# Layer 3's attention: scores and transposed probabilities share two alternating PSUM banks, and the tasks of a step run in another sequence

## The chip, the cores and the metric

The kernel runs on one core of one Trainium2 chip. The metric is the device time of one execution in microseconds (us). Six engine rows appear in the profile: PE (TensorE's matmuls), PEld (its weight loads), DVE (VectorE), ACT (ScalarE), POOL (GpSimd) and SP (which issues the transfers).

## The reference, cut to what matters

The program is a four-layer network over 16 batches of 128 tokens and 256 channels. The change touches layer 3's attention alone. It has two passes: `own` (keys and values from the tokens themselves) and `cross` (keys and values from a context). Each pass computes, for each batch:

```python
q = ln(fp8_linear(ln_out, wq))       # 16 heads of 128
k = ln(fp8_linear(ln_out, wk))       # 8 key heads of 128
v = fp8_linear(ln_out, wv)           # 8 value heads of 128
scores = einsum("bsghd,btgd->bghst", q, k) * d ** -0.5
p = softmax(scores)
core = einsum("bghst,btgd->bsghd", p, v)
x = x + fp8_round(core / proj_smooth) @ wproj * scale
```

In the cross pass k and v come from `cond @ w_kv_x` in float32. What follows layer 3's attention (a mixture of experts) starts when the cross pass has ended.

## The kernel before, in words

`stage_l3_attention` runs `Layer3Pass` twice, own and cross, each with a block of its own on all engines. A pass goes through its 16 batches in **steps**. One step works on four batches at once: `a`, the attention of batch n; `c`, centring, transposing and scaling the heads of batch n+1 and projecting its values; `p`, projecting queries and keys of batch n+2 and taking their statistics; `r`, rounding the rows of batch n+3. `steps` (L2882) gives each engine the tasks of one hand-written list, `OWN_ORDER` (L2735) or `CROSS_ORDER` (L2757), in the order of that list: an engine runs those that are its own, strictly in sequence, and waits on semaphores inside each. There are three steps that only fill the pipeline, then twelve in a hardware loop of two steps a turn (batches 0 to 11 at `a`), one more full one (batch 12), and then one without `r`, one without `p` as well, and one with `a` alone: 16 steps have an attention batch.

The attention of a batch is cut into four units u of four heads each. The chain of one unit goes: `scores` (L3030, PE, 8 matmuls into the PSUM bank `s_ps`), `maximum` (L3257, DVE), `exponential` (L3103, ACT, four heads), `normalise` (L3261, DVE), `turn_probs` (L3043, PE, four transposes into the bank `pt_ps`), `turned` (L3137, ACT, a copy to SBUF), `apply` (L3050, PE), `scale` (L3142, ACT), `round` (L3270, DVE, five instructions), `output` (L3058, PE, 12 matmuls). After four units `add` (L3281, DVE) adds the result to X. As there is one bank of each kind, scores of unit u wait for the exponential of unit u-1, and the transposes of unit u for `turned` of unit u-1:

```python
wait(pe, exp_ready, at_batch(b, U, u))        # scores
wait(pe, probst_ready, at_batch(b, U, u))     # turn_probs
```

The other tasks: `project` and `project_values` (L2989, L3005, PE into `p_ps`, two banks), `keep` and `keep_values` (L3113, L3119, ACT), `statistics` (L3227, DVE, four heads), `deviation` (L3232, DVE; it waits for the last centring of the batch before), `inverse` (L2944, POOL, a power and a product), `center` (L2952, POOL, five units of four heads), `center here` (L3249, DVE, the sixth unit), `turn_heads` (L3012, PE), `affine` (L3126, ACT), and in the own pass `rows`, `magic` and `quantise` (L3200, L3205, L3210, DVE) and `value` (L3083, ACT). In the own pass's last two steps `next weights` (L3164 and L3306) cuts eight tiles of the cross pass's weights into two parts each, ACT first, then DVE; SP loads a tile (`sp_load`, L2697) into one of two buffers when the tile two before it has been cut.

Of the kernel before, what the change touches and what calls it, by code (L numbers as in the profile page):

```python
# [22 lines left out]
P = 128  # L23
# [2700 lines left out]
class Layer3Pass:  # L2724
# [20 lines left out]
        ("a", "normalise", 2), ("p", "keep", 3), ("a", "scores", 3), ("a", "next weights", 1), ("a", "turn", 2),  # L2745
# [3 lines left out]
        ("a", "round", 1), ("c", "affine", 1), ("a", "next weights", 2), ("a", "apply", 2), ("p", "statistics", 3),  # L2749
# [7 lines left out]
    CROSS_ORDER = [  # L2757
        ("a", "scores", 0), ("a", "exponential", 0), ("a", "maximum", 0), ("c", "project values", 0),
        ("c", "keep values", 0), ("a", "normalise", 0), ("c", "project values", 1), ("c", "center", 0),
        ("c", "keep values", 1), ("a", "maximum", 1), ("a", "scores", 1), ("r", "value", 0), ("a", "turn", 0),  # L2760
        ("r", "quantise", 0), ("a", "turned", 0), ("p", "project", 0), ("a", "exponential", 1),
        ("c", "center here", 2), ("a", "apply", 0), ("p", "keep", 0), ("a", "normalise", 1), ("p", "project", 1),
# [704 lines left out]
```

## Time and profile before

| what | before |
|---|---|
| median of 3 runs (lowest to highest) | 2794.41 us (2784.98 to 2795.93) |
| the profiled execution | 2789.37 us, span 2787.6 us |
| PE busy over the span | 2289.0 us (82%) |
| DVE, ACT, POOL busy | 1831.1 (66%), 1524.3 (55%), 1515.2 us (54%) |
| last `add` of the own pass's batch 15 | at 1859.2 us of the span |
| last `add` of the cross pass's batch 15 | at 2335.7 us of the span |

The profile shows one execution; times in it count from the first instruction. Busy time counts what an engine executes, not its waits. In a timeline, idle time before an instruction is put down to what released it. The two passes of layer 3's attention lie between about 1325 and 2340 us.

### The profile page before, as it was taken

The page shows a single profiled execution, that of the slowest core. Times are in us where ns is not written, and L with a number is a line of the kernel's source. Part 1 is how long each engine was busy: PE and PEld are TensorE (multiplying, and loading weights), DVE is VectorE, ACT ScalarE, POOL GpSimd, SP SyncE. Part 2 cuts the span into 40 slices and gives each one's busy share as a digit, 9 for nine tenths or more (in the row PEclk, how much of TensorE's full clock was granted, in tenths as well). Part 3 has the DMA queues.
Part 4 walks back from the last instruction along what each step waited for, and adds up shares of the span by engine and source line. Part 5 has one row for each costly group of instructions (what it writes and reads, how often), then busy time and mean ns, then how long its engine had stood idle before and what let it go on. Part 6 is the DMA issues. An engine that isn't in the chain of part 4 may idle for free. (4 is left out here: it accounts for less than half of the span.)

```text
span 2787.6 us, 45731 instructions
## 1 busy us (share of the span) xinstructions
PE 2289.0 (82%) x14565; PEld 1664.4 (60%) x14574; DVE 1831.1 (66%) x3797; ACT 1524.3 (55%) x3405; POOL 1515.2 (54%) x1497
## 2 busy tenths in 40 slices
PE   4898244969889586897389999868999997999998
PEld 2333022548546343785267777757888886788886
DVE  3887585655547354455678888757888874666565
ACT  1677383752120265343478888757788773344443
POOL 5542104520002442583278888818888882888882
PEclk9999665989999799799699999988999996999999
DMA  5243103432040443232200000020000000343443
GB/s 135 68 97 69 50 0 91 148 121 110 4 187 1 105 93 89 84 101 68 94 1 0 0 0 0 7 78 7 4 6 6 2 2 30 100 116 111 117 115 82
DMA packets 119445, 174.20 MB, mean 62 GB/s; under 512 B 25597, under 2 KB 79005, under 8 KB 116207
## 3 DMA queue, kind: packets, MB, share of 16 engines
q1 hardware_dynamic: 118703, 171.58, 21.7%
q8 instruction: 91, 1.49, 0.2%
q10 hardware_dynamic: 576, 0.52, 0.1%
q14 instruction: 75, 0.61, 0.1%
HBM read 122.06 MB, written 11.48 MB: 48 GB/s over the span
## 5 line engine op out<-in xcount | busy, mean ns | idle before, releaser
L527 DVE TENSOR_REDUCE a_mraw<-a_wave_ps 128x4 f32<-128x1024 f32 (+1 forms) x256 | 308.4, 1218 | 118.6 <-PE a_wave_ps L359 115.2
L415 ACT ACTIVATE a_et<-a_wave_ps 128x1024 f32<-128x1024 f32 x256 | 262.9, 1028 | 113.9 <-PE a_wave_ps L376 110.6
L2956 POOL TENSOR_SCALAR a3o_raw<-a3o_raw,a3o_mu,a3o_dev 128x128 f32<-128x128 f32 x320 | 304.8, 967 | 5.4 <-issue 5.4
L2956 POOL TENSOR_SCALAR a3x_raw<-a3x_raw,a3x_mu,a3x_dev 128x128 f32<-128x128 f32 x320 | 280.2, 891 | 4.8 <-issue 4.8
L1755 DVE TENSOR_TENSOR f3e_hidden_low<-f3e_hidden,f3e_hidden_high 128x512 fp32r<-128x512 f32 x96 | 116.6, 1215 | 126.6 <-ACT f3e_hidden_high L1708 126.2
L393 PE MATMUL a_o_ps<-a_et,a_vt 128*32 128x256 f32 x2048 | 167.3, 400 | 26.1 <-ACT a_osb L445 24.4
L1616 POOL TENSOR_TENSOR f3e_product<-f3e_silu,f3e_up 128x512 f32<-128x512 f32 x96 | 143.6, 1499 | 72.0 <-PE f3e_u_ps L1635 43.0
L359 PE MATMUL a_wave_ps<-a_ks,a_qs 64*128 64x256 bf16 (+2 forms) x1280 | 121.3, 267 | 30.6 <-DMA a_ks<-a_parts 20.6
L1701 ACT ACTIVATE f3e_silu<-f3e_g_ps 128x512 f32<-128x512 f32 x96 | 57.4, 598 | 144.1 <-PE f3e_g_ps L1635 137.1
L2947 POOL TENSOR_TENSOR a3o_dev<-a3o_var,a3o_minus_half 128x24 f32<-128x24 f32 x16 | 68.9, 4304 | 118.7 <-DVE a3o_var L3247 118.7
L1749 DVE TENSOR_TENSOR f3e_hidden<-f3e_product,f3e_spread 128x512 f32<-128x512 f32 x96 | 124.6, 1298 | 6.7 <-DMA f3e_spread<-f3e_shares 6.6
L146 POOL TENSOR_TENSOR row_rstd<-row_var,row_half 128x14 f32<-128x14 f32 (+6 forms) x15 | 26.1, 1742 | 181.9 <-DVE row_var L141 181.9
L376 PE MATMUL a_wave_ps<-a_qs,a_ks 64*128 64x256 bf16 (+2 forms) x896 | 118.0, 298 | 4.6 <-DMA a_qs<-a_mt 2.8
L3108 ACT ACTIVATE a3x_weights<-a3x_s_ps,a3x_nmax 128x128 f32<-128x128 f32 x256 | 91.3, 379 | 42.1 <-DVE a3x_nmax L3259 42.0
L2947 POOL TENSOR_TENSOR a3x_dev<-a3x_var,a3x_minus_half 128x24 f32<-128x24 f32 x16 | 68.9, 4304 | 79.1 <-DVE a3x_var L3247 79.1
L359 PEld LDWEIGHTS a_wave_ps<-a_ks,a_qs 64*128 64x128 bf16 (+1 forms) x1280 | 64.6, 101 | 70.4 <-ACT a_et L415 23.9
L2986 PE MATMUL a3x_p_ps<-a_wkv,a3x_ctx_parts 128*128 128x512 f32 x384 | 103.6, 413 | 0.0
L3108 ACT ACTIVATE a3o_weights<-a3o_s_ps,a3o_nmax 128x128 f32<-128x128 f32 x256 | 93.3, 413 | 18.4 <-DVE a3o_nmax L3259 18.2
L2647 POOL TENSOR_TENSOR X<-X,f1c_kept 128x1024 f32<-128x1024 f32 x3 | 7.2, 2396 | 173.2 <-ACT f1c_kept L2640 173.2
L2986 PE MATMUL a3o_p_ps<-a_wq,a3o_xq 128*128 128x512 f32 x256 | 78.6, 440 | 26.8 <-ACT a3o_vv L3123 17.6
L376 PEld LDWEIGHTS a_wave_ps<-a_qs,a_ks 64*128 64x128 bf16 (+1 forms) x896 | 41.8, 96 | 93.9 <-issue 66.0
L3067 PE MATMUL a3x_o_ps<-a3x_wparts,a3x_catq 128*128 128x256 bf16 x768 | 96.2, 276 | 2.0 <-DVE a3x_catq L3279 2.0
(486 smaller groups left out, 6941.1 us busy)
## 6 DMA issues: line engine op xcount, KB each, us to landing
f_w<-in_f_w SPq DMA_DIRECT2D x16, 1216.0 KB, 8.6
a_qs<-a_parts SPq DMA_DIRECT2D x144, 128.0 KB, 2.4
f_raw<-in_f_w SPq DMA_DIRECT2D x60, 256.0 KB, 2.6
a_ks<-a_parts SPq DMA_DIRECT2D x96, 128.0 KB, 2.4
f3e_spread<-f3e_shares SPq DMA_DIRECT2D x64, 192.0 KB, 3.0
f2e_spread<-f2e_shares SPq DMA_DIRECT2D x36, 256.0 KB, 3.4
f3e_spread<-f3e_shares SPq DMA_DIRECT2D x64, 128.0 KB, 3.1
f_raw<-in_f_w SPq DMA_DIRECT2D x60, 128.0 KB, 2.8
```

The costliest lines, as they stand in the source:

```text
L359: last = nc.tensor.matmul(out[:, u, c * N:c * N + N], self.queries(p, self.ROWS, b, tq, rows), self.keys(p, self.ROWS, b, tk, slice(0, N)) ...
L376: last = nc.tensor.matmul(out, self.keys(p, self.ROWS_WITH_MAXIMA, b, t, rows), self.queries(p, self.ROWS_WITH_MAXIMA, b, tq, slice(0, N)) ...
L393: last = nc.tensor.matmul(self.o_ps[32 * j:32 * j + 32, columns], self.vt[:, b // 2 % self.NV, b % 2, c, self.block(k, j), :], self.et[:, ...
L415: self.nc.scalar.activation(self.et[:, g % self.WAVES_HELD, :, :], self.wave_ps[:, self.second_place[g][0], :, :], ACT.Exp, scale=self.sca ...
L527: v.tensor_reduce(out, wave.rearrange("p u (c n) -> p u c n", n=N), AX.X, ALU.max).then_inc(self.max_taken, 1)
L1616: nc.gpsimd.tensor_tensor(product[:, n % self.PRODUCTS, :], silu[:, n % 2, :], up[:, n % 2, :], ALU.mult).then_inc(product_ready, 1)
L1749: nc.vector.tensor_tensor(hidden[:, n % 3, :], product[:, n % self.PRODUCTS, :], spread[:, n % self.SPREAD, :], ALU.mult).then_inc(hidden_ ...
L1755: nc.vector.tensor_tensor(hidden_low[:, n % 2, :], hidden[:, n % 3, :], hidden_high[:, n % 2, :].bitcast(F32), ALU.subtract).then_inc(low_ ...
L2947: nc.gpsimd.tensor_tensor(dev[:, :], var[:, :], minus_half[:, :], ALU.pow)
L2956: mm = nc.gpsimd.tensor_scalar(head, head, mu[:, h:h + 1], dev[:, h:h + 1], ALU.subtract, ALU.mult)
L2986: mm = nc.tensor.matmul(out, lhs, rhs, start=(i == 0), stop=(i == len(pairs) - 1))
L3108: mm = nc.scalar.activation(weights[:, u % 2, h, :], s_ps[:, h, :], ACT.Exp, bias=nmax[:, u % 2, h:h + 1], accum_out=total[:, u % 2, h:h + 1])
```

## The change

The two banks `s_ps` and `pt_ps` become one tensor of two banks, `sp_ps`. Unit u uses bank u % 2, first for its scores, then for its transposed probabilities. Scores of units 0 and 1 have no wait for a bank; those of units 2 and 3 wait until `turned` of unit u-2 has copied the bank. The transposes lose their second wait: the bank's scores were read by the exponential that they wait for anyway.

```diff
-            s_ps = ps("s_ps", [P, 4, P])
-            pt_ps = ps("pt_ps", [P, 4, P])
+            sp_ps = ps("sp_ps", [P, 2, 4, P])
...
-                        wait(pe, exp_ready, at_batch(b, U, u))
+
+                        if u >= 2:
+                            pe.wait_ge(probst_ready, at_batch(b, U, u - 1))
                         for h in range(4):
-                            mm = nc.tensor.matmul(s_ps[:, h, :], qk[:, q, 4 * u + h, :],
+                            mm = nc.tensor.matmul(sp_ps[:, u % 2, h, :], qk[:, q, 4 * u + h, :],
...
                         pe.wait_ge(probs_ready, at_batch(b, U, u + 1))
-                        wait(pe, probst_ready, at_batch(b, U, u))
                         for h in range(4):
-                            mm = nc.tensor.transpose(pt_ps[:, h, :], weights[:, u % 2, h, :], ident[:, :])
+                            mm = nc.tensor.transpose(sp_ps[:, u % 2, h, :], weights[:, u % 2, h, :], ident[:, :])
```

`exponential`, `turned` and `maximum` read `sp_ps[:, u % 2, ...]` in the same way. Both order lists hold the same tasks as before in another sequence. Cut to its first and last lines, `OWN_ORDER` changes so:

```diff
-        ("a", "scores", 0), ("c", "keep values", 0), ("a", "maximum", 0), ("c", "project values", 0),
-        ("a", "exponential", 0), ("r", "rows", 0), ("c", "project values", 1), ("c", "center", 0),
...
-        ("p", "statistics", 5), ("a", "next weights", 3), ("a", "scale", 3), ("p", "inverse", 0), ("a", "output", 2),
-        ("p", "deviation", 0), ("c", "affine", 4), ("c", "turn", 5), ("a", "add", 0), ("c", "affine", 5),
-        ("a", "output", 3),
+        ("c", "project values", 0), ("a", "scores", 0), ("c", "keep values", 0), ("c", "project values", 1),
+        ("a", "scores", 1), ("c", "keep values", 1), ("a", "maximum", 0), ("p", "project", 0), ("a", "maximum", 1),
+        ("a", "exponential", 0), ("r", "rows", 0), ("r", "turn", 0), ("p", "project", 1), ("p", "keep", 0),
...
+        ("p", "statistics", 5), ("a", "next weights", 1), ("a", "output", 3), ("c", "affine", 5), ("p", "deviation", 0),
+        ("a", "add", 0), ("p", "inverse", 0), ("r", "quantise", 0), ("a", "next weights", 2), ("a", "next weights", 3),
```

What each engine runs in one step, read from the lists (st statistics, nw next weights, pv project values, kv keep values; PE's `turn` is of rows, heads or probabilities, here r-turn, h-turn, p-turn):

```
own, PE before:  scores 0, pv 0, pv 1, project 0, r-turn 0, scores 1, p-turn 0, project 1, r-turn 1, project 2,
                 scores 2, p-turn 1, h-turn 0, apply 0, project 3, scores 3, p-turn 2, apply 1, h-turn 1, project 4,
                 project 5, p-turn 3, apply 2, h-turn 2, h-turn 3, output 0, apply 3, output 1, h-turn 4, output 2,
                 h-turn 5, output 3
own, PE after:   pv 0, scores 0, pv 1, scores 1, project 0, r-turn 0, project 1, p-turn 0, project 2, apply 0,
                 p-turn 1, scores 2, project 3, r-turn 1, scores 3, apply 1, output 0, h-turn 0, p-turn 2, project 4,
                 apply 2, p-turn 3, output 1, h-turn 1, apply 3, h-turn 2, h-turn 3, project 5, output 2, h-turn 4,
                 h-turn 5, output 3
own, ACT before: kv 0, exponential 0, kv 1, keep 0, value 0, exponential 1, keep 1, turned 0, nw 0, keep 2, value 1,
                 exponential 2, ...
own, ACT after:  kv 0, kv 1, exponential 0, keep 0, exponential 1, turned 0, keep 1, keep 2, scale 0, turned 1,
                 value 0, exponential 2, scale 1, keep 3, exponential 3, turned 2, value 1, scale 2, turned 3,
                 affine 0, keep 4, affine 1, nw 0, scale 3, affine 2, keep 5, affine 3, affine 4, nw 1, affine 5,
                 nw 2, nw 3
own, DVE before: maximum 0, rows, normalise 0, maximum 1, st 0, center here, normalise 1, nw 0, st 1, maximum 2,
                 st 2, magic, normalise 2, nw 1, maximum 3, quantise, normalise 3, round 0, round 1, nw 2, st 3,
                 round 2, round 3, st 4, st 5, nw 3, deviation, add
own, DVE after:  maximum 0, maximum 1, rows, normalise 0, center here, normalise 1, st 0, st 1, st 2, maximum 2,
                 round 0, maximum 3, normalise 2, round 1, normalise 3, st 3, magic, round 2, nw 0, st 4, round 3,
                 st 5, nw 1, deviation, add, quantise, nw 2, nw 3
cross, PE after: scores 0, scores 1, pv 0, pv 1, project 0, p-turn 0, project 1, apply 0, scores 2, p-turn 1,
                 project 2, project 3, scores 3, project 4, apply 1, h-turn 0, p-turn 2, project 5, apply 2,
                 h-turn 1, h-turn 2, p-turn 3, output 0, apply 3, output 1, h-turn 3, output 2, h-turn 4, h-turn 5,
                 output 3
```

Before, the cross pass's PE began with scores 0, pv 0, pv 1, scores 1, p-turn 0. POOL's own sequence (centre the five units of `c`, then `inverse` of `p`) stays as it was.

## Rows read from the trace of the kernel before

**Rows 1.** Busy time by stretch: us, then PE, PEld, DVE, ACT, POOL busy, clock, DMA share
```profile
1401.42:1433.15 31.73, 30.18 (x182) 24.23 (x181) 23.43 (x77) 24.76 (x76) 22.76 (x22) 0.94 0.01 1
1433.15:1800.27 367.12, 346.13 (x2210) 276.04 (x2209) 305.95 (x982) 304.20 (x959) 306.09 (x286) 1.00 0.00 0
2014.22:2278.90 264.68, 263.33 (x1762) 227.84 (x1762) 214.83 (x710) 212.53 (x678) 219.03 (x220) 1.00 0.01 4
```

**Rows 2.** DVE's timeline, own pass: start us, us, instruction, idle before and releaser
```profile
1490.21 0.68 DVE L3259 TENSOR_REDUCE a3o_nmax<-a3o_s_ps 128x4 f32<-128x512 f32 x1
...
1492.46 0.18 DVE L3263 RECIPROCAL a3o_inv_total<-a3o_total 128x4 f32<-128x4 f32 x1 [1.25 <-ACT a3o_weights L3108]
...
1493.68 0.69 DVE L3259 TENSOR_REDUCE a3o_nmax<-a3o_s_ps 128x4 f32<-128x512 f32 x1 [0.27 <-PE a3o_s_ps L3039]
...
1496.33 0.18 DVE L3263 RECIPROCAL a3o_inv_total<-a3o_total 128x4 f32<-128x4 f32 x1 [0.16 <-ACT a3o_weights L3108]
...
1502.58 0.70 DVE L3213 TENSOR_TENSOR a3o_value<-a3o_value,a3o_magic 128x1024 bf16<-128x1024 bf16 x1
...
1504.53 0.17 DVE L3263 RECIPROCAL a3o_inv_total<-a3o_total 128x4 f32<-128x4 f32 x1
...
1514.32 1.64 DVE L3230 BATCH_NORM_STATS2 a3o_stats<-a3o_raw 128x6 f32<-128x128 f32 x8
1516.11 0.20 DVE L3236 TENSOR_TENSOR a3o_mu<-a3o_stats 128x24 f32<-128x24 f32 x1
...
1517.63 0.48 DVE L3283 SCALAR_TENSOR_TENSOR X<-a3o_o_ps,a3o_out_scale,X 128x256 f32 x1
1518.14 0.69 DVE L3259 TENSOR_REDUCE a3o_nmax<-a3o_s_ps 128x4 f32<-128x512 f32 x1
...
1521.33 0.18 DVE L3263 RECIPROCAL a3o_inv_total<-a3o_total 128x4 f32<-128x4 f32 x1 [2.19 <-ACT a3o_weights L3108]
```

**Rows 3.** POOL's timeline, own pass
```profile
1489.90 4.19 POOL L2947 TENSOR_TENSOR a3o_dev<-a3o_var,a3o_minus_half 128x24 f32<-128x24 f32 x1 [4.55 <-DVE a3o_var L3247]
...
1494.66 19.32 POOL L2956 TENSOR_SCALAR a3o_raw<-a3o_raw,a3o_mu,a3o_dev 128x128 f32<-128x128 f32 x20 [0.19 <-issue]
1517.72 4.19 POOL L2947 TENSOR_TENSOR a3o_dev<-a3o_var,a3o_minus_half 128x24 f32<-128x24 f32 x1 [3.75 <-DVE a3o_var L3247]
```

**Rows 4.** PE's timeline, own pass
```profile
1492.48 1.16 PE L3039 MATMUL a3o_s_ps<-a3o_qk 128*128 128x128 f32 x8 [0.39 <-ACT a3o_weights L3108]
...
1514.53 1.47 PE L3067 MATMUL a3o_o_ps<-a3o_wparts,a3o_catq 128*128 128x256 bf16 x12
1515.84 1.06 PE L3039 MATMUL a3o_s_ps<-a3o_qk 128*128 128x128 f32 x8
1516.65 2.10 PE L2986 MATMUL a3o_p_ps<-a_wkv,a3o_xq 128*128 128x512 f32 x8
```

**Rows 5.** ACT's timeline, own pass, start of a turn of the loop
```profile
1517.92 1.28 ACT L3123 ACT_TABLE_LOAD   x1 [2.42 <-PE a3o_p_ps L2986]
1519.22 0.69 ACT L3123 ACTIVATE a3o_vv<-a3o_p_ps,a3o_v_scale 128x512 f32<-128x512 f32 x1
1519.80 0.36 ACT L3108 ACTIVATE a3o_weights<-a3o_s_ps,a3o_nmax 128x128 f32<-128x128 f32 x1
...
1521.17 0.71 ACT L3123 ACTIVATE a3o_vv<-a3o_p_ps,a3o_v_scale 128x512 f32<-128x512 f32 x1
```

**Rows 6.** DVE's timeline, `add`: own pass batches 13, 15; cross pass 14, 15
```profile
1800.10 0.48 DVE L3283 SCALAR_TENSOR_TENSOR X<-a3o_o_ps,a3o_out_scale,X 128x256 f32<-128x256 f32 x1
...
1859.18 0.48 DVE L3283 SCALAR_TENSOR_TENSOR X<-a3o_o_ps,a3o_out_scale,X 128x256 f32<-128x256 f32 x1 [0.45 <-PE a3o_o_ps L3067]
...
2303.53 0.48 DVE L3283 SCALAR_TENSOR_TENSOR X<-a3x_o_ps,a3x_out_scale,X 128x256 f32<-128x256 f32 x1 [1.63 <-PE a3x_o_ps L3067]
...
2335.73 0.48 DVE L3283 SCALAR_TENSOR_TENSOR X<-a3x_o_ps,a3x_out_scale,X 128x256 f32<-128x256 f32 x1 [2.37 <-PE a3x_o_ps L3067]
```

**Rows 7.** DMA issues, 1770 to 1875 us: count, KB each, median us to landing
```profile
a_wraw<-in_a_cross_wkv SPq DMA_DIRECT2D x4, 512.0 KB, 4.0
```

**Rows 8.** One line of the kernel: `center`, ns min/median/max
```profile
L2956 POOL TENSOR_SCALAR a3o_raw<-a3o_raw,a3o_mu,a3o_dev x320: 787/906/2786, 1381.1 to 1823.0; 128x128 f32<-128x128 f32 x160
L2956 POOL TENSOR_SCALAR a3x_raw<-a3x_raw,a3x_mu,a3x_dev x320: 789/842/2882, 1887.3 to 2300.6; 128x128 f32<-128x128 f32 x160
```

**Rows 9.** PE's timeline, cross pass, last step (batch 15)
```profile
2307.88 2.05 PE L3039 MATMUL a3x_s_ps<-a3x_qk 128*128 128x128 f32 x8 [3.50 <-ACT a3x_weights L3108]
```

More of the change, by code:

```diff
@@ L2735 @@
     OWN_ORDER = [
-        ("a", "scores", 0), ("c", "keep values", 0), ("a", "maximum", 0), ("c", "project values", 0),
-        ("a", "exponential", 0), ("r", "rows", 0), ("c", "project values", 1), ("c", "center", 0),
-        ("c", "keep values", 1), ("a", "normalise", 0), ("p", "project", 0), ("p", "keep", 0), ("r", "turn", 0),
-        ("a", "maximum", 1), ("r", "value", 0), ("a", "scores", 1), ("p", "statistics", 0), ("a", "exponential", 1),
-        ("a", "turn", 0), ("c", "center here", 2), ("p", "keep", 1), ("p", "project", 1), ("c", "center", 1),
@@ L2741 @@
-        ("r", "turn", 1), ("a", "turned", 0), ("a", "normalise", 1), ("p", "project", 2), ("a", "next weights", 0),
[3 rows of a table removed]
-        ("a", "normalise", 2), ("p", "keep", 3), ("a", "scores", 3), ("a", "next weights", 1), ("a", "turn", 2),
[3 rows of a table removed]
-        ("a", "round", 1), ("c", "affine", 1), ("a", "next weights", 2), ("a", "apply", 2), ("p", "statistics", 3),
[3 rows of a table removed]
-        ("p", "statistics", 5), ("a", "next weights", 3), ("a", "scale", 3), ("p", "inverse", 0), ("a", "output", 2),
-        ("p", "deviation", 0), ("c", "affine", 4), ("c", "turn", 5), ("a", "add", 0), ("c", "affine", 5),
@@ L2755 @@
-        ("a", "output", 3),
+        ("c", "project values", 0), ("a", "scores", 0), ("c", "keep values", 0), ("c", "project values", 1),
+        ("a", "scores", 1), ("c", "keep values", 1), ("a", "maximum", 0), ("p", "project", 0), ("a", "maximum", 1),
+        ("a", "exponential", 0), ("r", "rows", 0), ("r", "turn", 0), ("p", "project", 1), ("p", "keep", 0),
+        ("a", "normalise", 0), ("a", "exponential", 1), ("c", "center", 0), ("c", "center here", 2), ("a", "turn", 0),
[10 rows of a table added]
+        ("c", "center", 5), ("c", "turn", 2), ("a", "next weights", 0), ("a", "scale", 3), ("c", "turn", 3),
@@ L2756 @@
+        ("p", "project", 5), ("p", "statistics", 4), ("c", "affine", 2), ("a", "round", 3), ("a", "output", 2),
+        ("p", "keep", 5), ("c", "affine", 3), ("c", "turn", 4), ("c", "turn", 5), ("c", "affine", 4),
+        ("p", "statistics", 5), ("a", "next weights", 1), ("a", "output", 3), ("c", "affine", 5), ("p", "deviation", 0),
+        ("a", "add", 0), ("p", "inverse", 0), ("r", "quantise", 0), ("a", "next weights", 2), ("a", "next weights", 3),
     ]
     CROSS_ORDER = [
-        ("a", "scores", 0), ("a", "exponential", 0), ("a", "maximum", 0), ("c", "project values", 0),
@@ L2759 @@
[L2759 to L2762, printed above, removed]
[13 rows of a table removed]
+        ("a", "scores", 0), ("a", "scores", 1), ("a", "maximum", 0), ("c", "project values", 0),
@@ L2776 @@
+        ("a", "exponential", 0), ("a", "maximum", 1), ("c", "project values", 1), ("c", "keep values", 0),
+        ("a", "normalise", 0), ("a", "exponential", 1), ("p", "project", 0), ("c", "center here", 2),
+        ("c", "center", 0), ("c", "keep values", 1), ("a", "turn", 0), ("a", "normalise", 1), ("p", "project", 1),
[14 rows of a table added]
     ]
@@ L3107, in exponential @@
                         for h in range(4):
-                            mm = nc.scalar.activation(weights[:, u % 2, h, :], s_ps[:, h, :], ACT.Exp,
+                            mm = nc.scalar.activation(weights[:, u % 2, h, :], sp_ps[:, u % 2, h, :], ACT.Exp,
                                                       bias=nmax[:, u % 2, h:h + 1],
@@ L3139, in turned @@
                         wait(act, applied, at_batch(b, U, max(u - 1, 0)))
-                        nc.scalar.copy(flat(probst[:, u % 2, :, :]), flat(pt_ps[:, :, :])).then_inc(probst_ready, 1)
+                        nc.scalar.copy(flat(probst[:, u % 2, :, :]), flat(sp_ps[:, u % 2, :, :])).then_inc(probst_ready, 1)
                     def scale(b, u):
@@ L3258, in maximum @@
                         dve.wait_ge(scored, at_batch(b, U, u + 1))
-                        v.tensor_reduce(nmax[:, u % 2, :], s_ps[:, :, :], AX.X, ALU.max, negate=True).then_inc(max_ready, 1)
+                        v.tensor_reduce(nmax[:, u % 2, :], sp_ps[:, u % 2, :, :], AX.X, ALU.max, negate=True).then_inc(max_ready, 1)
                     def normalise(b, u):
```

46 rows, old and new, of tables (CROSS_ORDER, OWN_ORDER) are left out of this document.

## The prediction, blind

> **What bounds the kernel now.** The change touches two passes, so I read first the busy time by stretch [rows 1]. One step of the own pass goes from one power on POOL to the next; the thirteen steps of batches 1 to 13 take 367.12 us, 28.24 each, and batch 0's takes 31.73. In none of them is an engine full by its busy time: PE 94%, DVE, ACT and POOL 83%. The cross pass is another case: in ten steps of it (264.68 us, 26.47 each) PE is busy for 263.33. The cross pass is bound by PE's own work and a wait removed there can give about 1.35 us in ten steps. What is to be had is in the own pass.
>
> Busy time hides the drains between dependent DVE instructions, so next I read DVE's timeline of one turn of the loop [rows 2]. From maximum 0 to the next maximum 0 are 27.93 us, in which DVE waits 1.25 + 0.27 + 0.16 = 1.68. DVE is thus occupied for 26.25 us of a step. The next step begins at 1518.14 and shows the same list with a wait of 2.19 in place of 1.25. The large waits are all of one kind: normalise waits for an exponential. PE at the same place waits for the same exponential before scores 1 [rows 4].
>
> POOL has a circle of its own [rows 3]: centring takes 19.32 us, ends at 1513.98, and the next power starts at 1517.72. Between them lies DVE's deviation, which began only at 1516.11 because statistics 4 and 5 came before it [rows 2]. Were it at once, the circle would be 19.32 for centring, 1.52 for deviation (1516.11 to 1517.63), and 4.76 from the power's start to the first centring (1489.90 to 1494.66): 25.6, with two semaphores 25.8. So the floors of an own step are DVE 26.25 and POOL 25.8. PE's floor is lower than either. The cross list runs dense in 26.47, and it has eight matmuls more than the own list (six instead of four for each of the four projections from the context); at 2.10/8 = 0.26 each [rows 4] the own list, with two small transposes more, is dense at 24.6.
>
> **The change, part by part.** *The banks.* Scores of units 0 and 1 no longer wait for an exponential. Scores 2 and 3 wait for `turned` of unit 0 and 1 instead, which in the new list lie at least three PE tasks ahead of them. Behind a scores that waits, PE holds a projection, and behind that ACT's keep and DVE's statistics. I cost the new waits at nothing: by the durations below turned 0 ends some 1.5 us before scores 2 is reached, turned 1 some 0.6 before scores 3. If the cover is gone, a wait costs PE a few tenths, and PE has 1.9 us to spare in a step of 26.5.
>
> *The sequence in the own pass.* I lay the new list out by start-to-start durations: two projections 2.1, scores 0.81 to 1.0 (I take 0.95), output 1.31 [rows 4]; exponential 1.37 [rows 5]; statistics 0.8, quantise 1.95, deviation 1.6, add 0.5, maximum 0.6 [rows 2]; a semaphore from PE to DVE about 0.25, since scores started at 1492.48 let maximum go at 1493.68 [rows 2, 4]. With PE's values 0 at 0, maximum 1 can start at 1.05 + 0.95 + 1.05 + 0.95 + 0.25 = 4.25. From there DVE runs the whole list to round 3 without another large wait: exponential 0 ends at about 5.3, when DVE has just finished rows, and is the one short wait (0.2); exponential 1 ends 0.3 before normalise 1 could start. That work is 26.25 less statistics 5, deviation, add, quantise and maximum 0, which run after round 3: 26.25 - 5.5 = 20.75. Then output 3, 0.1 + 1.31, and PE starts again. **T = 4.25 + 0.2 + 20.75 + 1.4 = 26.6 us.** DVE closes its own circle in the same time: after round 3 it has 5.5 us of work, while PE needs 1.4 + 4.25 to bring scores 1, so it idles 0.15. The quantise that now stands at the end is what fills that gap. Project 0 needs it and comes at 4.0; it is ready at about 3.4.
>
> *The table load.* Once a turn of the loop ACT loads a table for 1.28 us before keep values 0, and exponential 0 comes behind both [rows 5]; the wait of 2.19 in that step, against 1.25 in the other, shows 0.94 of it [rows 2]. In the new list ACT's first tasks are keep values 0 and 1, and exponential 0 is not due before 4.0. The load ends at 1.3 + 1.28 = 2.6, keep values 0 at 3.15, and keep values 1 has to wait for its matmuls until 3.3 anyway: the load costs nothing.
>
> The Trainium skill (ScalarE: Activation LUTs, "What ACT_TABLE_LOAD costs") adds a drain to it, 2.66 us for a switch. By that figure the load would put off exponential 0 by some 1.2 us in every second step of the loop, about 7 us in the pass. The trace speaks against it: keep values 0 starts at 1519.22, 1.30 us after the load does, and nothing is idle between them [rows 5].
>
> *Sum for the own pass.* Batches 1 to 13: 13 x (28.24 - 26.6) = 21.3, and batch 13's step, without rows and quantise, is held by POOL at 25.8, another 0.8: **-22**. Batch 0's step runs partly at a lower clock (0.94) [rows 1]; I leave 2.3 us of its excess, 31.73 - 29: **-2.7**. Before it, deviation no longer stands behind quantise, 1.95 us, which I count at half: **-1**.
>
> *The last two own steps.* They take 59.1 us [rows 6]. Here `next weights` moves most. Four tiles of a step were spread over it; now three of the four stand at its end, two of them behind add. A tile is loaded only when the tile two before is cut, and lands 4.0 us later [rows 7], so tiles 2 and 3 of batch 14's step cannot be cut before some 28 and 32 us after the step's start. ACT and DVE, in sequence, hold batch 15's exponential 0 behind that, some 7 us later than it could be. The same happens at the end of batch 15's step, with 4 to 6 us after add. Against it stands that the two steps' attention chain, which in the last step had nothing to hide its waits, gets shorter: scores 1 is ready with scores 0, and exponentials follow one another. Laid out task by task it comes to 58.5: **-1**, with -6 and +8 as ends.
>
> *The cross pass.* PE's list is again dense in my layout: scores 0 and 1, both values, project 0 (5.0) and turn of the probabilities at 6.0, when normalise 0 has long ended. T stays at PE's 26.35 to 26.45; fifteen steps give **-2**, the ends being -2 and, with half a microsecond of new waits a step, +7. In the last step a batch is alone, 32.2 us from add to add [rows 6], and PE waits 3.50 us for one exponential [rows 9]. The new list takes 23 us at the full clock and 32 at the lower one; half of that at either: **-4**, between 0 and -9.
>
> Sum: -22 - 2.7 - 1 - 1 - 2 - 4 = **-33 us**. The profiled execution took 2789.4, so 2756.4; the median of the runs shown is 5.0 above it. I forecast **2761 us**.
>
> **The rivals.** *A, the waits only move (0.15).* T of a step needs DVE without idle time, through some 28 tasks in fixed sequence. If three or four of them come half a microsecond late (most likely maximum 3, which stands behind round 0, and the exponential 3 and normalise 3 that hang on it), DVE idles its 1.7 us as before. Then 28.24 stays and only the ends give: 2789.4 - 8 + 5.0 = 2786. For it speaks that PE's slack of 1.9 is already split into short waits; against it, that in my layout normalise 3 stands behind a whole round 1, 1.4 us in which exponential 3 can be late.
>
> *B, the other side (0.07): POOL becomes the bound and gets slower.* The place is POOL's centring: a head takes 906 ns in the own pass and 842 in the cross pass, 787 at least [rows 8], and the own pass has more DVE work beside it. If a denser DVE stretched centring, the circle of 25.8 would grow by 20 times the stretch. It passes the forecast's 26.6 at 0.04 us a head, takes the whole gain at (28.24 - 25.8)/20 = 0.12, and at 0.2 a step takes 29.8, 1.6 more than now: 14 x 1.6 = +22, with the ends (-8) 2794.4 + 22 - 8 = 2808. The rows show a difference of 0.064 between the passes; at that the step is 27.1 and the time 2767.
>
> The Trainium skill (SBUF — State Buffer) calls the port that VectorE and GpSimd share an exclusive lock, held for a whole instruction. By that rule each DVE instruction that takes the lock costs POOL the same whether they lie dense or not, so a step's sum would not grow; no row before shows a denser step.
>
> *C, the ends give more (0.12).* The last steps gain 9 and 6, and steps run at 26.25: 2761 - 10 - 5 = 2746.
>
> *D, no effect of the banks.* PE's waits for the exponentials were covered and DVE is the bound whatever the banks do. Then the sequence alone gives the gain; the time is the same as in my forecast.
>
> **Chances.** My forecast, with D, 0.66; A 0.15; B 0.07; C 0.12. The range of 8 in 10 leaves out B's upper part and most of A's: 2745 to 2784. A measurement of this kernel can tell about 0.5%, 14 us, from no change. Faster by more than that, below 2780, is the forecast, C and a small part of B: 0.80. Within it: A and some of the forecast's upper tail, 0.15. Slower: B from about 0.2 us a head on, 0.05.
>
> **What would show it.** Steps of the own pass 26.3 to 26.9 us from power to power on POOL; DVE's idle before normalise 0 under 0.4 us with the table load too; no wait of scores 2 or 3 above a few tenths; centring near 19.3 us a step; POOL's wait for deviation near 2 instead of 3.75 and 4.55; cross steps 26.3 to 26.5; DVE and ACT waiting for a tile's load at the end of batch 14's step. Steps at 28 with new waits before maximum 3 or normalise 3 would make it wrong by A, centring above 21 us by B.

## The result, and the profile after

The changed kernel takes 2766.1 us in the median of 4 runs (2756.6 to 2769.3) against 2794.1 for the kernel before, measured beside it, a ratio of 0.9906 with a 95% interval of 0.988 to 0.9931. Forecast were 2761 and 2745 to 2784. A second measurement, beside an experiment below, gave 0.9903 (0.988 to 0.9926).

The profiled execution took 2756.6 us, 32.7 less than the one before; the sum of the prediction was 33. But the terms don't all agree, so the time is first cut up by markers in the two traces: POOL's power of each batch, the memset with which POOL opens a pass, and the first `row_rstd` after the passes.

| stretch | before | after | difference | forecast |
|---|---|---|---|---|
| own pass, start to power 1 | 81.44 | 81.67 | +0.2 | -1 |
| batch 0's step (power 1 to 2) | 31.64 | 28.31 | -3.3 | -2.7 |
| batches 1 to 13 (power 2 to 15) | 367.12 | 344.87 | -22.2 | -22 |
| power 15 to the cross pass's start | 61.90 | 66.63 | **+4.7** | -1 |
| cross pass, start to power 1 | 44.80 | 44.88 | +0.1 | 0 |
| cross pass, power 1 to 15 | 371.94 | 369.51 | -2.4 | -2 |
| cross pass, power 15 to the `row_rstd` | 58.83 | 53.51 | -5.3 | -4 |
| the two passes | | | **-28.3** | -33 |
| everything else | | | -4.4 | 0 |

The changed code does not run in the last row; a part of that size comes and goes between executions of one kernel (two profiled executions of the changed kernel have spans of 2754.9 and 2763.0 us, with the same steps in both passes). So the change itself gives 28 us, the difference of the medians, and the sum's agreement to 0.3 us is luck: one term is 5.7 us off, and 4.4 us that come and go hide it.

**The steady own step.** POOL's timeline of the kernel after, start and duration in us, then idle time and what ended it; the rows that answer to [rows 3]:

```profile
1481.73 4.19 POOL L2945 TENSOR_TENSOR a3o_dev<-a3o_var,a3o_minus_half 128x24 f32<-128x24 f32 x1 [2.98 <-DVE a3o_var L3246]
...
1486.48 18.03 POOL L2954 TENSOR_SCALAR a3o_raw<-a3o_raw,a3o_mu,a3o_dev 128x128 f32<-128x128 f32 x20 [0.19 <-issue]
1508.28 4.27 POOL L2945 TENSOR_TENSOR a3o_dev<-a3o_var,a3o_minus_half 128x24 f32<-128x24 f32 x1 [3.77 <-DVE a3o_var L3246]
```

From power to power are 26.55 us; before, two successive steps took 27.82 and 28.92. The two kinds of step, without and with ACT's table load, have become equal. POOL still waits 3 to 4 us in each: it has slack and is not the bound.

DVE's timeline of one step after, cut to its waits and its ends, answers to [rows 2]:

```profile
1484.22 1.29 DVE L3258 TENSOR_REDUCE a3o_nmax<-a3o_sp_ps 128x4 f32<-128x512 f32 x2
...
1486.48 0.18 DVE L3262 RECIPROCAL a3o_inv_total<-a3o_total 128x4 f32<-128x4 f32 x1 [0.64 <-ACT a3o_weights L3107]
...
1508.20 0.48 DVE L3282 SCALAR_TENSOR_TENSOR X<-a3o_o_ps,a3o_out_scale,X 128x256 f32 x1
1508.77 0.69 DVE L3212 TENSOR_TENSOR a3o_value<-a3o_value,a3o_magic 128x1024 bf16<-128x1024 bf16 x1
...
1512.98 0.18 DVE L3262 RECIPROCAL a3o_inv_total<-a3o_total 128x4 f32<-128x4 f32 x1 [0.48 <-ACT a3o_weights L3107]
```

Maxima 0 and 1 run back to back (x2) without a wait, which one bank would not allow, since scores 1 would wait there for exponential 0. The one wait above 0.25 us is normalise 0 for its exponential, 0.64 and 0.48, where it was 1.25 and 2.19. From 1486.48 to 1512.98 are 26.50 us with 0.48 of waiting: DVE is occupied for 26.0 of them.

The table load falls in the second of these steps. ACT's timeline, to hold beside [rows 5]:

```profile
1508.84 1.28 ACT L3122 ACT_TABLE_LOAD   x1 [1.30 <-PE a3o_p_ps L2984]
1510.13 1.26 ACT L3122 ACTIVATE a3o_vv<-a3o_p_ps,a3o_v_scale 128x512 f32<-128x512 f32 x2
```

The load delays keep values 0, the two keeps then run as one group, and DVE's wait behind them (0.48) is no longer than in the step without a load (0.64). The load costs nothing now. The Trainium skill (ScalarE: Activation LUTs, "What ACT_TABLE_LOAD costs") would add a drain of 1.38 us to each load; here the next instruction starts 1.29 us after the load does, and the idle time ahead of the load, 1.30, is that ahead of keep values 0 in the step without a load, 1.24, so the trace again does not show one.

PE's timeline of the same step, from the transposes of unit 1 on, shows the new waits for a bank:

```profile
1489.83 0.60 PE L3046 MATMUL a3o_sp_ps<-ident,a3o_weights 128*128 128x128 f32 x4
1490.26 1.06 PE L3039 MATMUL a3o_sp_ps<-a3o_qk 128*128 128x128 f32 x8
...
1492.21 1.06 PE L3039 MATMUL a3o_sp_ps<-a3o_qk 128*128 128x128 f32 x8
1493.10 1.03 PE L3053 MATMUL a3o_av_ps<-a3o_probst,a3o_vv 128*128 128x256 f32 x4
1494.54 1.48 PE L3066 MATMUL a3o_o_ps<-a3o_wparts,a3o_catq 128*128 128x256 bf16 x12 [0.41 <-DVE a3o_catq L3278]
```

Scores 2 and 3 (L3039) follow what stands ahead of them with no idle time. `turned` of unit 0 ends on ACT at 1488.80, 1.5 us before scores 2, as laid out.

**The last two own steps.** DVE's timeline of the kernel after, the end of batch 14's step and that of batch 15's, with the `add` of batches 13, 14 and 15 among the rows:

```profile
1773.24 0.48 DVE L3282 SCALAR_TENSOR_TENSOR X<-a3o_o_ps,a3o_out_scale,X 128x256 f32<-128x256 f32 x1
...
1801.00 0.48 DVE L3282 SCALAR_TENSOR_TENSOR X<-a3o_o_ps,a3o_out_scale,X 128x256 f32<-128x256 f32 x1
1801.94 1.28 DVE L2717 SCALAR_TENSOR_TENSOR a_wq<-a_wraw,a_in_scale,a_wq 128x1024 fp32r<-128x1024 f32 x1 [0.47 <-ACT a_wq L2708]
1806.17 1.28 DVE L2717 SCALAR_TENSOR_TENSOR a_wq<-a_wraw,a_in_scale,a_wq 128x1024 fp32r<-128x1024 f32 x1 [2.95 <-ACT a_wq L2708]
1807.38 1.28 DVE L3258 TENSOR_REDUCE a3o_nmax<-a3o_sp_ps 128x4 f32<-128x512 f32 x2
...
1831.73 0.48 DVE L3282 SCALAR_TENSOR_TENSOR X<-a3o_o_ps,a3o_out_scale,X 128x256 f32<-128x256 f32 x1 [0.45 <-PE a3o_o_ps L3066]
1833.14 1.22 DVE L2714 TENSOR_TENSOR a_wkv<-a_wraw,a_wkv 128x1024 fp32r<-128x1024 f32 x1 [0.93 <-ACT a_wkv L2706]
1836.32 1.23 DVE L2714 TENSOR_TENSOR a_wkv<-a_wraw,a_wkv 128x1024 fp32r<-128x1024 f32 x1 [1.95 <-ACT a_wkv L2706]
```

From the `add` of batch 13 to that of batch 15 are 58.49 us, 0.6 less than before [rows 6] and what the layout gave (58.5). But the pass does not end with the `add` any more: two tiles are cut behind it, and the last cut ends at 1837.55, 5.8 us after the `add` began. Before, the last cut stood ahead of the `add`. ACT's timeline says what each waited for:

```profile
1804.99 1.15 ACT L2708 ACTIVATE a_wq<-a_wraw,a_in_scale 128x1024 fp32r<-128x1024 f32 x1 [3.08 <-DMA a_wraw<-in_a_cross_wq]
...
1832.07 1.04 ACT L2706 CAST a_wkv<-a_wraw 128x1024 fp32r<-128x1024 f32 x1 [3.04 <-DMA a_wraw<-in_a_cross_wkv]
1835.24 1.04 ACT L2706 CAST a_wkv<-a_wraw 128x1024 fp32r<-128x1024 f32 x1 [2.13 <-DMA a_wraw<-in_a_cross_wkv]
```

A tile is asked for when the one two before it has been cut, so late cuts make late loads.

**The cross pass.** POOL's powers now come 26.16 and 26.53 us apart, before 26.39 and 26.56. PE is the bound here in both kernels; a window of ten steps before [rows 1] and one of nine steps after (us, then PE, PEld, DVE, ACT and POOL busy, clock, DMA share):

```profile
2022.10:2258.80 236.70, 235.87 (x1585) 206.80 (x1584) 191.71 (x639) 192.09 (x612) 200.81 (x199) 1.00 0.01 4
```

From the `add` of batch 14 to that of batch 15 were 32.20 us [rows 6] and are 26.18 (DVE's timeline, 2279.75 to 2305.93). The 3.50 us for which PE's scores 1 waited there [rows 9] are gone, but PE still sits idle for 3.50 us, now ahead of the first transposes. The clock changed too. The stretch from `add` to `add`, before and then after (columns as above):

```profile
2303.53:2335.73 32.20, 23.58 (x112) 18.56 (x110) 14.60 (x42) 12.53 (x52) 2.77 (x1) 0.65 0.00 1
```

```profile
2279.75:2305.93 26.18, 18.22 (x112) 14.55 (x110) 14.61 (x42) 12.37 (x52) 2.76 (x1) 0.87 0.00 1
```

The same 112 matmuls keep PE busy for 5.4 us less, at a granted clock of 0.87 instead of 0.65, and the stretch is 6.0 us shorter; PE's idle time falls only from 8.6 to 8.0 us. Most of the gain of this step thus lies in matmuls that ran faster. Why the clock is granted higher was not tried apart; it is 0.80 in `banks_only` (29.56 us) and 0.82 in `own_order_only` (28.34 us), which run the same cross pass, so 1.2 us of such a step also differ between runs of one code.

### The profile page after: what moved, and what is told of

It is laid out like the page before. It is cut to its first block and busy times, and to the rows that moved or that the text cites. A ratio compares the mean times of both kernels' runs of the same rounds, so it can differ in the third digit from the quotient of the medians.

```text
span 2754.9 us, 45640 instructions
## 1 busy us (share of the span) xinstructions
PE 2260.6 (82%) x14574; PEld 1654.5 (60%) x14574; DVE 1824.0 (66%) x3797; ACT 1525.5 (55%) x3405; POOL 1505.5 (55%) x1497
## 5 line engine op out<-in xcount | busy, mean ns | idle before, releaser
L2954 POOL TENSOR_SCALAR a3o_raw<-a3o_raw,a3o_mu,a3o_dev 128x128 f32<-128x128 f32 x320 | 291.8, 924 | 5.4 <-issue 5.4
L3107 ACT ACTIVATE a3x_weights<-a3x_sp_ps,a3x_nmax 128x128 f32<-128x128 f32 x256 | 90.7, 374 | 38.3 <-DVE a3x_nmax L3258 37.1
L3066 PE MATMUL a3o_o_ps<-a3o_wparts,a3o_catq 128*128 128x256 bf16 x768 | 94.6, 273 | 8.8 <-DVE a3o_catq L3278 8.7
L3107 ACT ACTIVATE a3o_weights<-a3o_sp_ps,a3o_nmax 128x128 f32<-128x128 f32 x256 | 93.4, 417 | 7.7 <-DVE a3o_nmax L3258 7.5
```

The costliest lines, as they stand in the source:

```text
L2954: mm = nc.gpsimd.tensor_scalar(head, head, mu[:, h:h + 1], dev[:, h:h + 1], ALU.subtract, ALU.mult)
L3107: mm = nc.scalar.activation(weights[:, u % 2, h, :], sp_ps[:, u % 2, h, :], ACT.Exp, bias=nmax[:, u % 2, h:h + 1], accum_out=total[:, u % ...
```

## The experiments

My theory was that own steps are bound by DVE's fixed list, that the new sequence with two banks takes DVE's waits out of it, and that PE's first four tasks and DVE's tail fit together to within a few tenths. Its rivals: the banks alone or the sequence alone do it; another engine is the bound; the sum of DVE's work bounds a step in any sequence. The kernel before took 2788.6 us beside the first four kernels, 2793.9 beside the next four, 2795.1 beside the last three. Step lengths are the distances of POOL's powers in the trace, in the loop; outside `order_only` they repeat to a few hundredths from one turn to the next.

### The banks alone

`banks_only`: the shared banks and their waits, both lists as before.

> The shared banks with both order lists of before. Theory (the banks only permit the new sequence): scores 1 may start about 0.4 us earlier, but maximum 1 stands behind normalise 0 in DVE's list, and normalise 0 waits 1.25 or 2.19 us for exponential 0 as before. Own step 28.0 to 28.4 us from power to power, cross step 26.4 to 26.5, last cross step 1 to 3 us shorter; total 0 to 8 us below the kernel before. Rival (the bank was the bottleneck): own step below 27.3, total 15 us or more below.

Measured: 2802.8 us, ratio 1.0048 (1.0033 to 1.0062), **slower** than the kernel before. Own steps take 28.52 and 29.59 us (+0.7), cross steps 26.82 and 27.01 (+0.4); only the last cross step gets shorter, 29.41 for 32.06 between its two `row_rstd`. Two groups of its waits, one turn of the loop (us in total, times, longest):

```profile
DVE a3o_inv_total L3263 <- ACT a3o_weights L3108: 4.4, 4, 2.1
...
PE a3o_sp_ps L3040 <- ACT a3o_probst L3140: 3.0, 4, 1.3
```

The second is the new wait, 1.3 us for scores 2 and 0.2 for scores 3 in the first step of the turn. Scores 2 wait for `turned` 0, which ACT runs behind exponential 1 and a keep, at 1502.13, 3.1 us after PE's transposes began. In the kernel after it starts 0.7 us after them (1488.21 for 1487.52), because scores 1 come early and exponential 1 is done by then. The first group holds normalise 0's wait, unchanged at 1.25 and 2.1 us, since the old list has only `rows` between maximum 0 and normalise 0, and normalise 1's, which grows from 0.16 to 0.52. With maxima 2 and 3, which wait 0.43 and 0.28 for their scores, DVE's waits in the first step sum to 2.48 us, where they were 1.68; these 0.8 us cover the 0.7 by which the step grew. Only the last cross step came as expected; the steady steps were outside both expectations, because the new waits cost something after all in the old list.

### The sequence alone

`order_only`: both new lists, the two banks as before, one of each kind.

> The two old banks, one for scores and one for transposed probabilities, with both new order lists. Theory: scores 1 now waits for exponential 0, and in the new list nothing of use stands in front of it. In the own pass maximum 1 comes at about 6.6 us of the step instead of 4.25, so a step takes 28.5 to 28.9; in the cross pass PE idles about 2.5 us per step, 28.8 a step. Total 2800 to 2845. Rival (the sequence alone gives the gain, the bank waits were covered): own step 26.6, total about 2766.

Measured: 2927.2 us, ratio 1.0489 (1.046 to 1.0518). The direction is my theory's and rival D of the prediction falls, but own steps take 31.0 to 33.9 us instead of under 29, cross steps 30.4 to 33.2, and the total lies 82 us above the expected band. Its waits from 1565 to 1700 us, the longest groups:

```profile
POOL a3o_dev L2946 <- DVE a3o_var L3246: 47.9, 5, 9.9
PEld a3o_s_ps L3038 <- ACT a3o_weights L3107: 24.5, 9, 3.0
DVE a3o_nmax L3258 <- PE a3o_s_ps L3038: 21.0, 9, 3.6
PE a3o_s_ps L3038 <- ACT a3o_weights L3107: 20.9, 9, 2.5
```

A list that puts scores 1 right behind scores 0 stops PE for a whole maximum and exponential (nine waits of up to 2.5 us), and DVE's maximum 1 and everything behind it with PE. The theory counted one such stop a step; there are two, scores 1 for exponential 0 (2.4 to 2.5 us) and scores 3 for exponential 2 (2.1 us). TensorE's granted clock also falls, to 0.95 over batches 1 to 13 (1435.51 to 1855.95 us), where the kernel after has 1.00. Behind one stop output 0 takes 2.77 us (PE's timeline, at 1614.56) where the kernel after takes 1.48. How the excess divides between stops and clock was not separated.

### The new own list, the old cross list

`own_order_only`: the shared banks, `OWN_ORDER` new, `CROSS_ORDER` as before.

> The shared banks in both passes and the new sequence in the own pass; the cross pass keeps its old list. Theory: 1 to 3 us slower than the changed kernel in the cross pass's steady part (26.45 against 26.35 a step) and some 3 us in its last step: 2768 to 2772. Rival (the cross pass gives a good part of the gain): 2776 or more.

Measured: 2774.0 us, ratio 0.9957 (0.9936 to 0.9977). Own steps are those of the changed kernel (26.55); cross steps take 26.79 and 26.97. The theory had the old cross list at 26.45 a step, 0.1 above the new; it is 0.5 above, so the total came out above the expected band and short of the rival's 2776. So in the cross pass the banks alone cost 0.4 us a step, the new list gives 0.5 to 0.6 back, and the net gain is the table's 2.43/14 = 0.17.

### Where the quantise stands

`quantise_mid`:

```diff
-("r", "magic", 0), ("a", "turned", 3), ("c", "affine", 0),
+("r", "magic", 0), ("r", "quantise", 0), ("a", "turned", 3), ("c", "affine", 0),
...
-("p", "inverse", 0), ("r", "quantise", 0), ("a", "next weights", 2), ("a", "next weights", 3),
+("p", "inverse", 0), ("a", "next weights", 2), ("a", "next weights", 3),
```

> The changed kernel with one task moved: in the own pass quantise (about 2 us of DVE) stands right behind magic instead of at the end of the step. My theory: behind the end of a step PE needs 1.4 us for output 3 and 4.25 us to bring scores 1, and the quantise at the end is what DVE does meanwhile; with it in the middle the stretch from maximum 1 to round 3 grows from 20.75 to about 22.7, so T = 4.25 + 0.2 + 22.7 + 1.4 = 28.5 us a step instead of 26.55, and the whole about 26 us above the changed kernel. Rival: a step is bound by the sum of DVE's work alone (26.25), then it stays at 26.5 to 26.7 wherever quantise stands.

Measured: steps of 28.18 and 28.32 us, 1.70 longer; 2784.8 us, ratio 0.9973 (0.9953 to 0.9993). DVE's timeline shows it standing idle where the quantise was:

```profile
1520.30 0.69 DVE L3258 TENSOR_REDUCE a3o_nmax<-a3o_sp_ps 128x4 f32<-128x512 f32 x1 [0.47 <-PE a3o_sp_ps L3039]
1522.12 0.69 DVE L3258 TENSOR_REDUCE a3o_nmax<-a3o_sp_ps 128x4 f32<-128x512 f32 x1 [1.13 <-PE a3o_sp_ps L3039]
```

The same work in another place costs 1.7 us a step, and the sum of DVE's work, which is unchanged, cannot be what bounds a step in any sequence. Nearly all of the own pass's gain hangs on one task of 2 us that fills the gap while PE brings the scores. The total is 18.7 us above the changed kernel's first measurement, less than the 26 of the theory, as a step took 28.25 and not 28.5, and batch 13's step has no quantise to move (25.9 us).

### More work on each engine in turn

Each is the changed kernel with one piece of work more in the own pass: in `dve_more` in the statistics of round 5, in `pool_more` ahead of the end of the first centred unit, in `pe_more_early` ahead of project values 1, in `pe_more_late` ahead of project 3. None of the added results is used.

```diff
+if own and r == 5:
+    v.bn_stats(spare[:, h, :], raw[:, parity(b), 4 * r + h, :])
...
+if own and m == 0:
+    nc.gpsimd.tensor_scalar(spare[:, :], ident[:, :], 2.0, None, ALU.mult)
...
+if own and r == 1:
+    product(p_ps[:, r, :], b, 2, wkv, slice(512 * (r + 2), 512 * (r + 3)))
...
+if own and r == 3:
+    product(p_ps[:, r % 2, :], b, 0, wq, slice(512 * r, 512 * r + 512))
```

> The changed kernel with the four statistics instructions of round 5 of the own pass done twice (0.8 us more DVE work in every step, in its tail behind round 3). My theory (both chains, PE to DVE to PE and DVE's own sum, are within 0.15 us of each other): the step grows from 26.55 to about 27.3, 14 steps by 0.8, 11 us in all. Rival, POOL bounds the step now (centring, power and the wait between them): deviation comes 0.8 later and the step grows by 0.8 too only if POOL's wait for deviation is the bound; if DVE has slack, 0.

> The changed kernel with one more instruction of the size of a centred head on POOL in every step of the own pass (0.8 to 0.9 us, result unused). My theory: POOL waits 2.98 and 3.77 us for deviation in each step, so the extra work is taken out of that wait and the step stays within 0.2 us of 26.55. Rival (POOL's circle bounds the step since the change): 0.8 to 0.9 more a step, 12 us in all.

> The changed kernel with the product of project values 1 done twice in every step of the own pass, 1.05 us more for PE ahead of scores 1. My theory: this lies on the chain that closes the step (PE's 4.25 us to scores 1, then DVE's 20.75), so the step grows by about 0.9 to 1.05, to 27.5, 13 to 15 us in all. Rival (DVE's own sum bounds the step, PE's path to scores 1 has room): at most 0.2 us a step.

> The changed kernel with the product of project 3 done twice in every step of the own pass: 1.05 us more for PE in the middle of the step, between turned 1 and scores 3. My theory: DVE's list from maximum 1 to round 3 bounds the step and PE has slack here, so at most 0.2 us a step where the same work ahead of scores 1 cost 0.64; scores 3 and with it maximum 3 come 1 us later, which DVE covers with round 0. Rival (PE's in-order list bounds the step wherever the work stands): again 0.6 a step, 9 us in all.

| kernel | work added | own step | grew by | us, ratio (interval) |
|---|---|---|---|---|
| changed kernel | | 26.55 | | |
| dve_more | 0.8 | 27.33 | 0.78 | 2776.3, 0.9929 (0.99 to 0.9959) |
| pool_more | 0.54 | 26.76 | 0.21 | 2771.2, 0.9904 (0.9882 to 0.9927) |
| pe_more_early | 1.05 | 27.20 | 0.65 | 2774.3, 0.9928 (0.9909 to 0.9948) |
| pe_more_late | 1.05 | 27.38 | 0.83 | 2777.3, 0.9943 (0.9914 to 0.9972) |

Work on DVE goes in one for one. POOL's added instruction took 0.54 us and not the 0.8 to 0.9 of its expectation. Its wait for deviation shrinks by 0.46 in the mean, and still the step grew by 0.21, just outside the 0.2 expected for a larger piece of work. Rival B's 0.8 to 0.9 did not come, but what passes 0.21 on to the step wasn't tried. POOL's timeline in `pool_more`:

```profile
1516.35 4.20 POOL L2946 TENSOR_TENSOR a3o_dev<-a3o_var,a3o_minus_half 128x24 f32<-128x24 f32 x1 [3.35 <-DVE a3o_var L3249]
...
1543.12 4.20 POOL L2946 TENSOR_TENSOR a3o_dev<-a3o_var,a3o_minus_half 128x24 f32<-128x24 f32 x1 [2.48 <-DVE a3o_var L3249]
```

For PE ahead of scores 1 the theory is right in kind: 0.65 of 1.05, so that path has 0.4 of room. In the trace maximum 1 now waits 1.04 and 0.77 us for its scores, and normalise 0's wait shrinks to 0.2. For PE in the middle the theory is wrong, and 0.83 is the size of the rival. What I had overlooked is that apply 1 stands behind project 3 too. DVE's timeline of `pe_more_late` shows one wait that the changed kernel doesn't have, round 1 for scale 1:

```profile
1525.08 0.29 DVE L2662 TENSOR_SCALAR a3o_cat<-a3o_cat 128x512 bf16<-128x512 bf16 x1 [0.34 <-ACT a3o_cat L3148]
```

That is 0.34 of 0.83. The rest lies in DVE's instructions, which follow one another at slightly larger distances over the step (from statistics 3 to the quantise 10.33 to 10.36 us for 10.00 to 10.09); why wasn't tried, so the rival's mechanism is shown for 0.34 only. The changed list is tight in more than one place.

### Other places for the cut of the tiles

`weights_spread` and `weights_early` move the four `next weights` of the changed own list. The first has number 0 ahead of maximum 2, 1 behind exponential 3, 2 ahead of round 2 and 3 ahead of affine 4. The second:

```diff
+("r", "value", 0), ("a", "next weights", 0), ("a", "maximum", 2),
...
+("a", "normalise", 3), ("a", "next weights", 1), ("c", "center", 4),
...
+("p", "statistics", 5), ("a", "next weights", 2), ("a", "output", 3), ("c", "affine", 5), ("p", "deviation", 0),
+("a", "next weights", 3), ("a", "add", 0), ("p", "inverse", 0), ("r", "quantise", 0),
```

> The changed kernel, with the four next-weights tasks spread over the step again, near the places they had before (ahead of maximum 2, behind exponential 3, ahead of round 2, ahead of affine 4). They do work in batches 14 and 15 only. Theory: from batch 13's add to the last cut tile the changed kernel takes 64.3 us where the kernel before takes 59.6, because batch 15's maximum 0 stands 6 to 7 us behind two tile loads. Spread, it comes to 54 to 58 us: total 6 to 10 us below the changed kernel, 2756 to 2760. Rival (the lower clock in these steps is the cause, not the place of the tiles): within 2 us of the changed kernel.

> The changed kernel with the four next weights of the own pass in other places: number 0 ahead of maximum 2 and number 1 behind normalise 3, where DVE and ACT were seen idle in the last two steps (3.38 and 5.12 us, 1.08 and 0.94 us), number 2 behind statistics 5, number 3 ahead of add. Steps 0 to 13 stay at 26.55 us. My theory: what the changed kernel lost between batch 13's step and the cross pass (66.63 us, before 61.90) is that tiles 2 and 3 are asked for late, since a tile is loaded only when the one two ahead of it is cut: 3.1 us of waiting before batch 15's maxima and 5.8 us behind its add. With these places the first shrinks to nothing and the second to nothing, against 1 to 3 us of DVE's and ACT's own time moved into the chain: 66.63 falls to 58 to 62, the whole by 5 to 8 us. Rival (the cost is the lower TensorE clock and in-order queues in the two lone steps, as spreading them otherwise, at 68.50, suggested): 65 or more.

`weights_spread` took 2767.3 us, ratio 0.9916 (0.9889 to 0.9944), and its stretch from power 15 to the cross pass 68.50 us instead of 66.63: a miss, by the number of its rival. No cut waits long for its load, but rounds 2 and 3 now stand behind cuts in DVE's sequence, and the outputs behind them. The clock fell as well, to 0.80 over the stretch where the changed kernel has 0.85, and PE is busy in it for 45.70 us instead of 39.61; this run doesn't separate the two. `weights_early` took 2760.2 us, ratio 0.9888 (0.9865 to 0.9911), beside 2764.9 and 0.9903 for the changed kernel once more:

> The changed kernel once more, beside weights_early on the same chip: 26.55 us a step, 66.63 us from batch 15's power to the cross pass, and a ratio of 0.990 to 0.991 to the kernel before by every theory.

Its stretch is 60.48 us, in the expected band, and the 66.63 of the changed kernel came out as 67.21 the second time. DVE's timeline of `weights_early` at the two ends:

```profile
1804.67 0.47 DVE L3282 SCALAR_TENSOR_TENSOR X<-a3o_o_ps,a3o_out_scale,X 128x256 f32<-128x256 f32 x1
1805.06 1.27 DVE L3258 TENSOR_REDUCE a3o_nmax<-a3o_sp_ps 128x4 f32<-128x512 f32 x2
...
1829.23 2.35 DVE L2714 TENSOR_TENSOR a_wkv<-a_wraw,a_wkv 128x1024 fp32r<-128x1024 f32 x2
1831.50 0.48 DVE L3282 SCALAR_TENSOR_TENSOR X<-a3o_o_ps,a3o_out_scale,X 128x256 f32<-128x256 f32 x1
```

The maxima of batch 15 follow batch 14's `add` at once, and nothing is left behind the last `add`. Cut up by the same markers, in us:

| | changed | weights_early | difference |
|---|---|---|---|
| `add` of batch 13 to that of 14 | 27.76 | 30.84 | +3.1 |
| `add` of 14 to the maxima of 15 | 6.38 | 0.39 | -6.0 |
| maxima of 15 to its `add` | 24.35 | 26.44 | +2.1 |
| `add` of 15 to the cross pass | 8.31 | 2.98 | -5.3 |

Both waits shrink as the theory said, by 11.3 us together; the cuts in their new places cost 5.2 us of it, more than the 1 to 3 expected. The stretch is 6.2 us shorter than in the changed kernel; the medians differ by 4.7, with intervals that overlap, so it is the trace that shows the gain. It is the best version of the study.

## Why the prediction was right, and where it wasn't

**Steady own step: right.** 26.6 was laid out, 26.53 is the mean of the thirteen. The parts are a little off both ways: DVE waits about 0.5 us for the exponential, not 0.2, and is occupied for 26.0, not 26.25. It is DVE's own circle that closes the step; maximum 1 waits for its scores in one step of two, and there for under 0.1 us, and PE's path has 0.4 us of room by `pe_more_early`, where the layout gave 0.15. Batch 13's step took 26.23 us and not POOL's 25.8. The 1.9 us that PE was to have to spare are not free where they were needed: 1.05 us more in the middle of its list cost 0.83. `dve_more` and `quantise_mid` show the two halves of the layout: DVE's work in the list counts in full, and the quantise at the end covers PE's way to the scores. Rival A (waits only move, 2786) did not come: there is no wait before maximum 3 or normalise 3.

**New waits at nothing: right for these lists only.** In the old lists they cost part of 0.7 us an own step and 0.4 a cross step. The cover named, three PE tasks ahead of the scores, is not what makes the difference: the old own list also has three PE tasks between the transposes of unit 0 and scores 2, and in `banks_only` PE waits there for up to 1.3 us. What the new list adds is on ACT: exponential 1 is done early, so nothing holds up `turned` 0. Banks alone lose 14 us by the medians, the sequence alone 139, both together gain 28. Rival D (the banks have no effect) falls, although its time was the forecast's: the time couldn't tell them apart, the runs did.

**Table load at nothing: right** by the waits of 0.48 and 0.64 with and without it.

**Batch 0's step: right** (-3.3 for -2.7). **Deviation before it: not seen**, +0.2 for -1; the first stretches hardly moved.

**The last two own steps: wrong, +4.7 for -1.** The layout of the two batches was good (58.5 against 58.49, and 59.02 in the second execution of the changed kernel, so the agreement to 0.1 us is partly luck). The step that failed is the sum: it compared `add` to `add`, and left out the 4 to 6 us of cuts behind batch 15's `add` that the same paragraph named. They measure 5.3 more than before (5.8 from the `add`'s start to the end of DVE's work, before 0.5). -0.6 + 5.3 is the +4.7. The marker must be the last thing that the next stage waits for, which was the `add` before and no longer is. `weights_early` confirms it, since moving those cuts ahead of the `add` gives the time back.

**The cross pass: right** in size, -2.4 for -2 and -5.3 for -4. PE bounds its steady steps. The -4 was the middle between a step at the full clock and one at the lower; which of them would come was not argued, and the clock makes most of the difference (0.65 before, 0.87 after).

**Rival B (POOL becomes the bound): wrong** in sign. Centring did not get slower beside denser DVE work: 921 ns a head in the thirteen steps, before 968. POOL waits 3 to 4 us a step, more than the 2 that I had named as a sign, and takes 0.54 us more work for 0.21 of the step. **Rival C (ends give more, 2746)** did not come: the cross end gave 5.3 of its 9, the own end lost.

## What to carry to other kernels

A second buffer and a new sequence are one change: the buffer without the sequence put a new wait, for the bank's last reader, beside the old one, and the sequence without the buffer stopped PE twice a step. When engines run fixed lists, lay out the closing gap of the loop (who waits for whom from the last task to the first) and put work there that nobody needs soon; one task of 2 us in that place was worth 1.7 us a step. At the end of a pass, measure up to the last thing that the next pass waits for, and look where prefetch work stands in the steps that have nothing else to hide it.

## What was not expected of the hardware

POOL's centring and DVE share the work on the same heads, and in the denser own step POOL was faster, not slower. The group of the 260 centred heads of batches 1 to 13 (busy us, mean ns), first of the kernel before, then after:

```profile
L2956 POOL TENSOR_SCALAR a3o_raw<-a3o_raw,a3o_mu,a3o_dev 128x128 f32<-128x128 f32 x260 | 248.1, 968 | 4.7 <-issue 4.7
```

```profile
L2954 POOL TENSOR_SCALAR a3o_raw<-a3o_raw,a3o_mu,a3o_dev 128x128 f32<-128x128 f32 x260 | 236.2, 921 | 4.7 <-issue 4.7
```

The step's DVE work is the same in both. In the cross pass the same group, of the 280 heads between powers 1 and 15, went the other way, from 889 to 901 ns, so the direction is not general. The Trainium skill (SBUF — State Buffer) has GpSimd and some DVE instructions, those with two inputs in SBUF among them, take turns at a shared port for whole instructions. With the same instructions in both kernels that alone gives no 0.9 us less a step, unless it matters which of them meet, and that wasn't tried.

The last steps ran at a lower TensorE clock after an idle stretch. PE's timeline of the kernel after, batch 15's step:

```profile
1810.63 1.11 PE L3046 MATMUL a3o_sp_ps<-ident,a3o_weights 128*128 128x128 f32 x4 [8.59 <-DVE a3o_weights L3265]
1812.42 2.07 PE L3053 MATMUL a3o_av_ps<-a3o_probst,a3o_vv 128*128 128x256 f32 x4 [0.68 <-ACT a3o_probst L3139]
...
1815.14 2.84 PE L3039 MATMUL a3o_sp_ps<-a3o_qk 128*128 128x128 f32 x16
```

After 8.59 us without work apply 0 takes 2.07 us (1.03 at the full clock of the step above) and the two scores 2.84 for 1.95; the granted clock from `add` to `add` (1801.00 to 1831.73) is 0.83. In `weights_early` PE waits 4.49 us at the same place, apply 0 takes 2.07 us again and the two scores 2.45, at 0.87 from `add` to `add` (1804.67 to 1831.50). Half the idle time thus cost apply 0 as much and the scores 0.4 us less. The late tile cost above all its wait; of the 6.2 us that `weights_early` gives back, these slower matmuls show 0.4.
